# A second key buffer, the context energy on TensorE, and the second layernorm's variance from ScalarE squares

## The reference

```python
x = layernorm(x + autocorrelation_attention(x))       # the lag 0 term rules; a guard on the other lags decides
sim = softmax(einsum('ncs,nds->ncd', ctx, x) * 256 ** -0.5, axis=1)
x = layernorm(x + einsum('ncd,nds->ncs', sim, ctx))    # the cross attention
out = x @ W_base.T + moe_lora(x)                       # top 2 of 8 experts of rank 8
x = layernorm(x + out)
```

## Time and profile before

| | us |
|---|---|
| median of the runs | 2191.81 |
| profiled execution, its own time | 2195.65 |
| its span, first to last instruction | 2193.8 |
| TensorE busy over the span | 1990.9 (91%) |
| VectorE, ScalarE, GpSimd busy | 988.7, 511.9, 296.7 |
| TensorE begins slot 0, about | 74 |
| end of the last context product | 708.7 |
| feed-forward's first matmul | 732.5 |

### The profile page before, as it was taken

How to read it: one execution, slowest core, us unless ns; L and a number is a source line. 1 busy time by engine, 2 the same in 40 slices (tenths; PEclk the granted TensorE clock), 3 DMA queues, 4 the chain that set the end, 5 groups by cost and what they waited for, 6 DMA issues and landing times.

```text
span 2193.8 us, 27988 instructions
## 1 busy us (share of the span) xinstructions
PE 1990.9 (91%) x11232; PEld 1056.9 (48%) x11232; DVE 988.7 (45%) x2182; ACT 511.9 (23%) x691; POOL 296.7 (14%) x418
## 2 busy tenths in 40 slices
PE   1878878878888699999999999999999999999998
PEld 1655645555555344444444444444444444444443
DVE  3788878888887652232223222232223222232222
ACT  4445444544442540010001000010001000110000
POOL 1242243243242320000000000000000000000000
PEclk9999999998999799999999999999999999999999
DMA  7588678778866752232223322232223322232220
GB/s 250 135 220 256 215 205 241 245 198 233 251 184 191 256 158 58 59 105 65 57 57 91 81 58 57 65 103 62 57 57 96 76 57 57 71 100 59 57 58 39
DMA packets 288907, 271.13 MB, mean 124 GB/s; under 512 B 261504, under 2 KB 261632, under 8 KB 265984
## 3 DMA queue, kind: packets, MB, share of 16 engines
q1 hardware_dynamic: 288832, 270.17, 42.4%
HBM read 138.02 MB, written 67.11 MB: 94 GB/s over the span
## 4 chain that ended last, share of the span: by engine, by line
PE 64%; ACT 1%; DMA 1%; POOL 1%; DVE 0%; issue 0%; ACTq 0%; SPq 0%; POOLq 0%
PE ps_y_f L1097 59%; PE ps_a_f L1116 1%; PE ps_y_f L1101 1%; PE ps_y_f L1102 1%; DMA chunk<-w_chunks 1%; PE ps_a_f L1117 1%; ACT w_hi_f L892 1%; POOL w_lo_f L875 0%; POOL chunk L874 0%; DVE w_lo_f L966 0%; PE ps_h_f L1124 0%; PE ps_t_f L1082 0%; DVE b_stack_f L1052 0%; ACT y_f L953 0%; ACT b_stack_f L950 0%
## 5 line engine op out<-in xcount | busy, mean ns | idle before, releaser
L1097 PE MATMUL ps_y_f<-w_hi_f,x_hi_f 128*128 128x512 f16 x2048 | 777.8, 380 | 9.9 <-POOL w_lo_f L875 7.4
L1097 PE MATMUL ps_y_f<-w_hi_f,x_lo_f 128*128 128x512 f16 x2048 | 778.0, 380 | 0.0
L1097 PE MATMUL ps_y_f<-w_lo_f,x_hi_f 128*128 128x512 f16 x2048 | 777.9, 380 | 0.0
L953 ACT ACTIVATE y_f<-y_f,nb_f,rs_f 128x2048 f32<-128x2048 f32 x32 | 67.0, 2093 | 1112.4 <-POOL nb_f L883 1112.4
L1097 PEld LDWEIGHTS ps_y_f<-w_hi_f,x_hi_f 128*128 128x128 f16 x2048 | 200.7, 98 | 246.8 <-POOL w_lo_f L875 9.6
L1097 PEld LDWEIGHTS ps_y_f<-w_hi_f,x_lo_f 128*128 128x128 f16 x2048 | 200.8, 98 | 242.6 <-issue 1.6
L1097 PEld LDWEIGHTS ps_y_f<-w_lo_f,x_hi_f 128*128 128x128 f16 x2048 | 200.7, 98 | 233.9 <-issue 1.4
L977 DVE SCALAR_TENSOR_TENSOR y_f<-ps_y_f,w_iscale,xn_f 128x512 f32<-128x512 f32 x64 | 46.6, 749 | 476.9 <-PE ps_y_f L1102 476.9
L977 DVE SCALAR_TENSOR_TENSOR y_f<-ps_y_f,w_iscale,xn 128x512 f32<-128x512 f32 x64 | 46.6, 748 | 447.9 <-PE ps_y_f L1102 447.9
L610 PE MATMUL ps_t_fast<-ident,xbuf_fast 128*128 128x128 f32 x512 | 95.5, 334 | 134.1 <-ACT xbuf_fast L413 116.3
L880 POOL TENSOR_TENSOR var_eps_f<-mv_f,columns 128x1 f32<-128x1 f32 x32 | 6.1, 191 | 1356.9 <-DVE mv_f L1065 1356.9
(11 more groups left out here) (146 smaller groups left out, 2055.2 us busy)
## 6 DMA issues: line engine op xcount, KB each, us to landing
cbuf_fast<-ctx_in SPq DMA_DIRECT2D x32, 1024.0 KB, 6.1
xbuf_fast<-x SPq DMA_DIRECT2D x32, 1024.0 KB, 8.8
x_scratch<-x2buf_fast SPq DMA_DIRECT2D x32, 1024.0 KB, 11.7
out<-y_f SPq DMA_DIRECT2D x32, 1024.0 KB, 4.1
xn<-w_chunks SPq DMA_DIRECT2D x16, 1024.0 KB, 8.4
xn<-x_scratch SPq DMA_DIRECT2D x16, 1024.0 KB, 4.8
xn_f<-x_scratch SPq DMA_DIRECT2D x16, 1024.0 KB, 4.8
chunk<-w_chunks SPq DMA_DIRECT2D x18, 512.0 KB, 5.6
```

What stands on the lines that cost most here:

```text
L953: nc.scalar.activation(y[parity][:], y[parity][:], ACT.Identity, bias=nb_[:, 0:1], scale=rs[:, 0:1]).then_inc(out_ready, 1)
L1097: nc.tensor.matmul(ps_y[j][:], xx[parity][:, k], ww[:, k, j * BANK:(j + 1) * BANK], start=(k == 0 and xx is x_hi and ww is w_hi), stop=False)
```

## The change

It does the following, all in `attention_pass` and its buffers:

- The keys have two buffers, and the transposes for batch n+2 are issued in slot n, at its end; stores, weights and rows are issued first. Context n+3 follows each low half.
- The sum over partitions of the context's sums of squares is a TensorE matmul with a matrix of ones, issued at j = 6, in place of GpSimd's partition all-reduce. VectorE reads it right after the banks.
- The first norm's small steps and its application go by halves, both applications on ScalarE, the second one behind the second exponential.
- The second norm: the context sums on VectorE also give their row sums (an accumulated output); VectorE makes the negative mean; ScalarE squares x2 minus its mean over 2048 columns with an accumulated output; GpSimd makes the variance and applies the norm, half 0 in slot n and half 1 in slot n+1.
- The weight squares move to the slot's end on ScalarE and write in place; several buffers share memory (`cbuf0` with two prefetched chunks, `u_t` with `ag_raw`), with two waits on SyncE's queue ahead of the load of `ag_raw`.

```diff
-        cbuf = sb("cbuf", [P, R, L], F32)
+        cbuf = [consts["cbuf0"], sb("cbuf1", [P, L], F32)]
-        k_both = sb("k_both", [P, KT, 2, C], F16)
+        k_both = [sb(f"k_both{i}", [P, KT, 2, C], F16) for i in range(2)]
+        sumall = ps_s[1][:, C:C + PIECES]
...
                         if (part, r) == (0, 0):
-                            after(sp, sim_done, R * n)
+                            after(sp, sim_done, R * (n - 1))
...
-                        transpose_keys(n + 1, 1 - parity, 0, 0)
-                        transpose_keys(n + 1, 1 - parity, 0, 1)
-                        for r in range(R):
-                            transpose_keys(n + 1, 1 - parity, 1, r)
-                            load_context(n + 2, r)
+                        store(n - 1, 1 - parity)
                         load_weights(n + 2)
-                        store(n - 1, 1 - parity)
                         load_x(n + 2, parity)
+                    for r in range(R):
+                        transpose_keys(n + 2, parity, 0, r)
+                    for r in range(R):
+                        transpose_keys(n + 2, parity, 1, r)
+                        load_context(n + 3, r)
...
+                sp.wait_ge(fwd_done, 4 * nb)
+                sp.wait_ge(vlo_done, R * nb)
                 sp.dma_start(consts["ag_raw"][:], ag_in.rearrange("p k c -> p (k c)")).then_inc(prefetched, 16)
...
+                def norm2(n, parity, r):
+                    at = slice(r, r + 1)
+                    pool.wait_ge(ssq2_ready, R * n + r + 1)
+                    after(pool, x2_ready, R * (n - 1) + r + 1)
+                    chain.link(g.tensor_tensor(var_eps[1][:, at], ssq2[parity][:, at], columns[:, ONE_LTH, at], ALU.mult))
+                    chain.link(g.tensor_tensor(var_eps[1][:, at], var_eps[1][:, at], columns[:, EPS_AT, at], ALU.add))
+                    chain.link(g.tensor_tensor(rs2[:, at], var_eps[1][:, at], columns[:, MINUS_HALF, at], ALU.pow))
+                    g.tensor_tensor(nb2[:, at], nmean2[parity][:, at], rs2[:, at], ALU.mult).then_inc(ln2_ready, 1)
...
-                    reduce_context()
+                    if is_batch(n - 1, nb):
+                        norm2(n - 1, 1 - parity, 1)
+                        normalise2(n - 1, 1 - parity, 1)
+                    if cur and n < nb - 1:
+                        norm2(n, parity, 0)
+                        normalise2(n, parity, 0)
+                    fold(0)
+                    norm1(0)
+                    fold(1)
+                    norm1(1)
...
+                    def spread2(n, parity, r):
+                        act.wait_ge(mean2_ready, R * n + r + 1)
+                        after(act, ssq2_ready, R * n + r)
+                        nc.scalar.activation(junk2[:], x2buf[parity][:, r], ACT.Square, bias=nmean2[parity][:, r:r + 1],
+                                             accum_out=ssq2[parity][:, r:r + 1]).then_inc(ssq2_ready, 1)
...
                         emptied_bank(j)
+                        if j == 1 and is_batch(n - 1, nb):
+                            spread2(n - 1, other, 1)
+                        if j == 5 and cur:
+                            spread2(n, parity, 0)
                         if 1 <= j <= PIECES:
                             square_context(j - 1)
-                        if j >= 6 and not (isinstance(n, int) and n == -2):
-                            square_weights(j - 6)
...
-                    normalise1()
+                    normalise1(0)
+                    square_weights(0)
+                    square_weights(1)
                     softmax_exp(1)
+                    normalise1(1)
...
-                                                   ALU.add).then_inc(ctx_added, 1)
-                            if j:
-                                x2_stats(j - 1)
+                                                   ALU.add, accum_out=x2sum[:, j:j + 1]).then_inc(ctx_added, 1)
+                            if j == NBANK:
+                                x2_mean(0)
...
+                    def context_energy():
+                        if n2:
+                            pe.wait_ge(sumsq_done, PIECES * (n + 3))
+                            if n == -2:
+                                pe.wait_ge(w_summed, 2)
+                            after(pe, scale_ready, n + 2)
+                            nc.tensor.matmul(sumall, ones[:], sumsq[parity][:], start=True, stop=True).then_inc(sumall_done, 1)
...
+                        if j == 6:
+                            context_energy()
```

More of the change, by code:

```diff
@@ L46 @@
 AG = ER + EXPERTS
-EPS4_AT, EPS_AT, MINUS_ONE, MINUS_HALF = range(4)
+EPS4_AT, EPS_AT, MINUS_ONE, MINUS_HALF, ONE_LTH = range(5)
 GUARD_GAP = 110.0
@@ L148, in attention_pass @@
         inv = sb("inv", [P, 4, BANK], BF16)
-        junk, junk_w = sb("junk", [P, HALF], BF16), sb("junk_w", [P, HALF], BF16)
+        junk2 = sb("junk2", [P, L], BF16)
+        junk = sb("junk", [P, HALF], BF16)
         stats = sb("stats", [P, R, NBANK, 6], F32)
-        stats2 = sb("stats2", [P, R, NBANK, 6], F32)
+        x2sum = sb("x2sum", [P, R * NBANK], F32)
         mv1 = sb("mv1", [P, R, 2], F32)
-        mv2 = sb("mv2", [P, R, 2], F32)
+        nmean2 = [sb(f"nmean2{i}", [P, R], F32) for i in range(2)]
+        ssq2 = [sb(f"ssq2{i}", [P, R], F32) for i in range(2)]
         rs1, nb1 = sb("rs1", [P, R], F32), sb("nb1", [P, R], F32)
@@ L320, in fold @@
                     def fold(r):
                         if n2:
+                            if r == 0:
+                                after(pool, t_filled, TB * (n + 1) + ORDER.index("u1") + 1)
                             pool.wait_ge(x_loaded[parity][r], 16 * (half + 2))
@@ L354, in slot @@
-                    if cur and not (isinstance(n, int) and n == nb - 1):
-                        pool.wait_ge(ln2_ready, n + 1)
-                        settle(1)
-                        for r in range(R):
-                            g.tensor_scalar(x2buf[parity][:, r], x2buf[parity][:, r], rs2[:, r:r + 1], nb2[:, r:r + 1], ALU.mult,
-                                            ALU.add).then_inc(x2_ready, 1)
-                    if isinstance(n, int) and n == nb - 1:
-                        pool.wait_ge(w_summed, 1)
+                            pool.wait_ge(mv1_ready, R * (n + 2) + r + 1)
@@ new lines, in norm1 @@
+                            after(pool, x1_ready[r], n + 2)
+                            norm_steps(slice(r, r + 1))
+                    if is_batch(n - 1, nb):
[7 more added lines that the diff above has]
+                    fold(1)
@@ L510, in slot @@
                         emptied_bank(p)
[L511 to L518 removed]
+                    if n2:
+                        dve.wait_ge(sumall_done, n + 3)
+                        chain.link(v.tensor_reduce(tmp[:, 0:1], sumall, AX.X, ALU.add))
+                        scale_steps(nc, chain, scale[parity][:], iscale[parity][:], tmp[:, 0:1], tmp2[:, 0:1])
+                        v.tensor_scalar(lscale[parity][:], iscale[parity][:], C ** -0.5, None, ALU.mult).then_inc(scale_ready, 1)
+                    if cur:
+                        x2_mean(1)
                     def value_low(r):
@@ L638, in logits @@
                             k = i // 3
-                            ins = nc.tensor.matmul(ps_s[r][:, 0:C], qq[:, k, r * P:(r + 1) * P], k_both[:, k, part, :],
+                            ins = nc.tensor.matmul(ps_s[r][:, 0:C], qq[:, k, r * P:(r + 1) * P], k_both[other][:, k, part, :],
                                                    start=(i == 0), stop=(i == 3 * KT - 1))
@@ L1416, in decoder_layer @@
             fwd_dram=fwd_dram, inv_dram=inv_dram, ident_dram=ident_dram, expert_dram=expert_dram)
+        halves = consts["cbuf0"][:].rearrange("p (h k c) -> p h k c", h=2, k=KC)
+        consts["chunks"] = [halves[:, 0], halves[:, 1], consts["chunk2"][:]]
         flag = sb("flag", [P, 1], I32)
```

129 lines of the change are left out of this document (50 added, 79 removed).

## The result

| | before | after |
|---|---|---|
| median of the runs | 2191.99 us (2190.49 to 2195.47) | 2078.11 us (2076.74 to 2081.09) |
| ratio to before | 1 | 0.948, 95% interval 0.9464 to 0.9497 |
| profiled execution, span | 2195.65, 2193.8 | 2078.46, 2076.6 |
| one slot, start to start, mean of 14 | 42.0 us | 34.36 us |
| TensorE busy and idle in it | 34.0, 8.0 us | 31.8, 2.6 us |

What follows compares the result with a forecast made beforehand. The prediction took GpSimd's partition all-reduce, delaying the fold, first norm and next slot, as the bound. Slots 80 plus head 16.5 minus seam 1 gave 95.5 us off, about 2096 us; range 2078 to 2136.

Steps and rivals of the forecast that it cites:

- the step that failed: At each slot's head: GpSimd's all-reduce costs 15 us per slot; fold, norm and next slot's start hang behind it.
- theory K: Formed after first runs: ring of transposes, context load, squares, copies, similarity closes at 40 us or more with one key buffer.
- Rival C: GpSimd's gap belongs to the fold, not the all-reduce: slots some 40 us, near 2150 us; chance 0.05 with the rest.
- my main case: The forecast outcome for the whole kernel: slots of 35.7 to 37.3 us, 2083 to 2110 us; chance 0.55.
- The slot: The 14 slots start to start: from 42.0 to 36.3 us, 5.7 us each, 80 us in all.
- the clock: TensorE at a slot's head: without idle the clock stays up, about 1 us per slot, 14 us, left out of sum.
- rival D: Better than forecast: slots of 35.2 us with the head of slots at full clock, 112 us off, 2080 us; chance 0.07.
- my terms (-0.8, +1.1, +0.3, +0.2): Bank phase per slot, us: bank waits -0.8, bank 3 behind ScalarE +1.1, the product +0.3, the probabilities +0.2.
- The head: Work before slot 0: without the all-reduce gaps slot 0 begins near 58 us, not 74.4; 16.5 us, bounds 10 and 23.
- The seam: Last slot: squares and chained steps replace statistics, the kept all-reduce starts 1 us later: +1 us, bounds 0 and +4.
- A: ScalarE's added 6.5 us delays bank evacuations: slots of 38.5 us, some 2130 us; chance 0.25 shared with B.
- B: Ring of SyncE's queue, squares and product: 36.4 or 38 us with slow transposes, 2120 us; chance 0.25 shared with A.

Runs made afterwards that it cites:

- the filler run: Kernel before with 16 more 512-column matmuls in TensorE's idle time at each slot's head: 2196.33 us, ratio 1.0007.
- the product with two keys: Kernel before with the TensorE energy product in place of the all-reduce and with two key buffers: 2142.0 us, ratio 0.9763.
- the kernel with VectorE's statistics: Changed kernel with the second norm's variance from VectorE's batch statistics again, without ScalarE's squares and accumulators: 2119.52 us, ratio 0.9661.

## Why the prediction came out as it did

**The cause: the step that failed.** "So the all-reduce ... costs GpSimd 15 us per slot, and the fold, the norm and the start of the next slot hang behind it" is right about GpSimd and about who waits, and wrong about what the slot's length hangs on. Taken out alone it leaves 42.2 us. The chain that I followed back from TensorE through line 413 to the all-reduce goes on: the all-reduce waits for the squares, these for the second context half, this for SyncE's transposes, and these for the similarity. In the slot of the earlier trace rows (from 369.1) the similarity before it ends at 362.05 and the high transposes go out at 362.09; the squares end at 384.1, line 413 at 411.73, and the similarity after that at 444.91. These are two slots in one turn, 82.9 us, 41.4 each. The first and last links (SyncE, TensorE; the squares, the all-reduce and line 413 stand in the earlier trace rows):

```profile
362.09 4.57 SPq L245 DMA_TRANSPOSE k_both_fast<-v_hi_fast  x2
...
375.45 0.57 SPq L237 DMA_DIRECT2D cbuf_fast<-ctx_in  x1
...
444.64 0.27 PE L639 MATMUL ps_s_fast<-k_both_fast,q_lo_fast 128*128 128x256 f16 x1
```

Without the all-reduce that long way is cut and the short one, theory K's, remains, at 42; without the wait for the buffer both are cut, as the run with two key buffers alone bears out. I stopped at the all-reduce because its 15 us were the most conspicuous part of the turn. I had seen that the second buffer removes the wait and gave it 0.8 us of bank waits; by itself it is worth 46 us. Rival C (the gap belongs to the fold) was wrong in its mechanism too: without the all-reduce the folds have no such gap.

**Why the sum came near all the same.** It named the state after the change and not the shares: idle time gone, TensorE's work left. For that state it is of no matter which ring was the longer, since the change opens both. That the time falls inside the range, by 0.1 us, is luck all the same: my main case (2083 to 2110 us, chance 0.55) did not come about, the one under 2083, to which I gave 0.07, did, and a miss of 27 us in the slots was made smaller by one of 6 us the other way in the head. The shares are not additive: the product is worth 5 us at the start of the table above and 125 us at its end. In part that is because a stall is paid for only when nothing longer covers it, in part because the rest of the change puts more of ScalarE's work on the ring of the all-reduce (15.9 us without idle time against 10.1 us of work, above).

**The slot: 36.3 forecast, 34.36 measured, 107 us instead of 80.** Idle time fell by 5.4 us, where my 5.7 was nearly all idle time. The mis-sized term is the clock, which I left out of the sum at 14 us: TensorE's busy time fell by 2.2 us a slot, 31 us. Before, the clock was at 0.50 for 5 us at the head of the next slot, from 411 to 416, and its mean over the 14 slots 0.93; now all slots read 1.00, and the slots of the filler run that kept 1.00 show that the clock alone takes busy time from 34.0 to some 32.0 us. With the ring closed that saved no time, as the same run shows; that it is time now that the ring is open is argued, from TensorE being busy for 93% of a slot. "TensorE: Matmul & The Clock Gate" of the Trainium skill (Part 1) has the clock fall after idleness; the trace before agrees, 0.50 behind 6.1 us of idle time. The clock was the term of rival D, whose 35.2 us slots and 2080 us came nearest.

**Smaller terms.** Bank phase: idle 3.58 us before (19.90 us with 16.32 busy, 369.1 to 389.0), 2.30 after, so -1.3 where my terms (-0.8, +1.1, +0.3, +0.2) made +0.8. The fourth bank waits 0.62 us, not 1.1. The product is two matmul records, 0.28 us together, where I took 0.3:

```profile
320.80 0.28 PE L612 MATMUL ps_s_fast<-sumsq_fast,ones_fast 128*128 128x4 f32 x2
```

It never waits for its squares outside the head. VectorE's accumulator read is 0.08 us eight times, 0.64 a slot, between my bounds of 0 and 1.5 and below ScalarE's 0.19 us each. The Trainium skill (VectorE: DVE Perf Modes, section "Two Vector instructions with no wait between them") counts such an op as two instructions; the trace agrees, with one read of 0.08 us behind each sum. The DMA share is 0.93 to 0.99 in slots 1 to 13, over the 0.88 I named, and 1 MB a slot less gained nothing.

**What VectorE's relief was worth.** I counted it as covers: 1.1 us of g_lags, nothing for line 577. The runs put some 40 us on the variance and, between the product with two keys and the kernel with VectorE's statistics, 22 us on the split norm with the rest (the orders of GpSimd, ScalarE and SyncE). The bound behind the ring was VectorE with 35.2 us, which I never listed, since at 42 us it showed idle time.

**The head: 16.5 forecast, 10.65 measured.** TensorE starts at 22.88 (21.5 forecast), but in slot -1 the queue is slower than the medians that I took the earlier trace rows: the two high transposes take 7.18 us and the last low one 5.20, the context half goes out at 33.00, and its squares hold the copies (lines at 16.78 to 33.00, TensorE's waits of 3.94, 3.99 and 3.61 us):

```profile
16.78 7.18 SPq L247 DMA_TRANSPOSE k_both_fast<-v_hi_fast  x2
...
27.76 5.20 SPq L247 DMA_TRANSPOSE k_both_fast<-v_lo_fast  x1
33.00 0.58 SPq L239 DMA_DIRECT2D cbuf_fast<-ctx_in  x1
```

Slot 0 begins at 63.75 us, not 58.

**The seam and what I left out.** Slot 14 is 1.45 us shorter; from its end to the first feed-forward matmul it is 0.3 us longer (+1 forecast); the feed-forward part is 1.95 us longer, with TensorE's wait for GpSimd's weight halves at 10.6 us. In the spans: 107.3 + 10.65 + 1.45 - 0.3 - 1.95 = 117.2.

**Rivals.** A (ScalarE's order) is there in small: 16.9 us behind line 391. B (the queue ring), 26.6 us a slot at the medians, did not bind after the change; a ring over the same transposes and context half, but closed by the single key buffer and the similarity, is what bound the kernel before. No run shows the turn to slower that it named.

**Left open.** Why the stores' later start by 0.5 us gains more than holding them until the half has landed: in the second case other waits grow, and no run splits the two effects. The shares within the 22 us weren't measured with two key buffers, and no run tests by itself that VectorE is the bound behind the ring.

## What to carry to other kernels

Follow the chain back until it closes on itself one iteration earlier: a wait that explains a gap is a cause only if nothing equally long feeds it. For every single buffer in a pipeline ask which transfer stands behind its release, and what stands behind that one in the same queue; then list the bounds behind the first (here 42 us for the ring, 38 for VectorE, 34 for TensorE), for each part of a change is worth only the distance to the next one. Ask too whether a part lengthens another ring, as ScalarE's added work did for the all-reduce. Weigh a move by the state it leads to, and don't split the sum among its parts without a run for each.

## What the runs showed of the hardware

GpSimd stood idle for 5.8 to 10.4 us before and 6.7 to 9.6 us after a 128-partition all-reduce of 0.44 us (the four traces that have it in the slots), with other neighbours on either side too. A DMA share of 0.93 to 0.99 in a slot did not bound it: 1 MB less left the time at 2079. Two stores issued right behind a 1 MB load moved its landing from 5.5 to 6.8 us (medians). An idle TensorE kept at work for 3.62 us a slot held its clock at 1.00 in ten of 14 slots, and the kernel took as long as before. The sum output of a VectorE pass left a record of its own, of 0.08 us.
